# Normalising an attention head and adding it to the residual: one VectorE product and one GpSimd addition against eight fused VectorE operations

## What is computed

```
q, k, v = x @ Wq + bq, x @ Wk + bk, x @ Wv + bv            # (b, n, 8 heads, 64)
scores  = einsum('bihd,bjhd->bhij', q, k) / sqrt(64) + mask
weights = softmax(scores, axis=-1)
out     = einsum('bhij,bjhd->bihd', weights, v).reshape(b, n, 512)
x       = layernorm(x + out)
```

## Time and profile before

| | us |
|---|---|
| median of 3 runs | 2533.32 (2531.81 to 2533.53) |
| profiled execution, its own time | 2532.79 |
| its span, first to last instruction | 2530.8 |
| PE busy | 2431.8 (96%) |
| DVE busy | 2215.7 (88%) |
| POOL busy | 1474.6 (58%) |
| ACT busy | 1331.1 (53%) |
| clock granted to PE, mean | 0.982 |

### The profile page before, as it was taken

One profiled execution on the slowest core, in us unless ns is written; L12 is line 12 of the kernel. 1 busy time (PEld: TensorE's weight loads), 2 busy tenths in 40 slices (PEclk: granted clock), 3 DMA queues, 4 the chain that ended last, 5 costly groups with the idle time before them and its releaser, 6 DMA issues. The chain is left out here.

```text
span 2530.8 us, 55069 instructions
## 1 busy us (share of the span) xinstructions
PE 2431.8 (96%) x15497; PEld 2070.5 (82%) x15497; DVE 2215.7 (88%) x6933; ACT 1331.1 (53%) x4104; POOL 1474.6 (58%) x1806
## 2 busy tenths in 40 slices
PE   4899999999999999999999999999999999999983
PEld 3688888888888888888888888888888888888873
DVE  6889889889999999998998988988999999998862
ACT  3355555555555555555555555555555555555542
POOL 5655566566565665655656656656656566565531
PEclk7899999999999999999999999999999999999996
DMA  4255666666566666666566566666666666666564
GB/s 130 59 130 138 141 139 139 140 138 141 137 140 138 141 140 141 136 143 145 129 141 145 134 144 141 138 141 139 141 137 137 141 140 139 139 138 140 129 127 100
DMA packets 1382908, 342.56 MB, mean 135 GB/s; under 512 B 1084880, under 2 KB 1347152, under 8 KB 1382864
## 3 DMA queue, kind: packets, MB, share of 16 engines
q1 hardware_dynamic: 1382864, 342.05, 59.4%
HBM read 174.13 MB, written 167.77 MB: 135 GB/s over the span
## 5 line engine op out<-in xcount | busy, mean ns | idle before, releaser
L901 PE MATMUL rot<-w_hi,y_hi 128*128 128x512 f32 x1024 | 416.3, 407 | 2.7 <-DVE y_lo L818 2.0
L903 PE MATMUL rot<-w_hi,y_lo 128*128 128x512 f32 x1024 | 404.1, 395 | 0.0
L902 PE MATMUL rot<-w_lo,y_hi 128*128 128x512 f32 x1024 | 402.7, 393 | 0.0
L508 ACT ACTIVATE probs<-score,sc_nmax 128x128 f32<-128x128 f32 x1024 | 361.3, 369 | 27.4 <-DVE sc_nmax L671 23.5
L381 POOL TENSOR_TENSOR ve<-mv,eps_col 128x1 f32<-128x1 f32 (+1 forms) x448 | 130.2, 291 | 345.1 <-DVE mv L663 247.7
L411 POOL TENSOR_TENSOR x2b<-x,bias 128x512 f32<-128x512 f32 x128 | 165.9, 1296 | 265.5 <-DVE x L762 265.5
L671 DVE CUSTOM_DVE_ANT_0 score<-score,mask 128x128 f32<-128x128 f32 x1024 | 259.6, 315 | 1.3 <-PE score L1000 1.3
L406 POOL TENSOR_TENSOR x<-x,o_norm 128x512 f32<-128x512 f32 x128 | 165.5, 1293 | 156.1 <-DVE o_norm L716 156.1
L693 DVE CUSTOM_DVE_ANT_0 dot_tmp<-x,u 128x512 bf16<-128x512 f32 x256 | 244.8, 992 | 11.8 <-ACT x L615 7.3
L421 POOL TENSOR_SCALAR e<-e 128x512 f32<-128x512 f32 x128 | 246.3, 1924 | 13.7 <-ACT e L568 13.7
L386 POOL TENSOR_TENSOR rs<-ve,half_neg 128x1 f32<-128x1 f32 (+1 forms) x448 | 249.2, 570 | 0.6
(11 more groups left out here) (119 smaller groups left out, 7051.8 us busy)
## 6 DMA issues: line engine op xcount, KB each, us to landing
pt_hbm<-probs SPq DMA_DIRECT2D x512, 128.0 KB, 2.8
probs_t<-pt_hbm SPq DMA_DIRECT2D x128, 512.0 KB, 4.0
x_in<-in_x SPq DMA_DIRECT2D x128, 256.0 KB, 4.0
xt_hbm<-x_b SPq DMA_DIRECT2D x512, 64.0 KB, 2.3
xt_f<-xt_hbm SPq DMA_DIRECT2D x128, 256.0 KB, 2.8
ot_hbm<-o_t SPq DMA_DIRECT2D x512, 64.0 KB, 1.9
o_norm<-ot_hbm SPq DMA_DIRECT2D x128, 256.0 KB, 2.7
out_x<-x SPq DMA_DIRECT2D x128, 256.0 KB, 2.4
```

Source lines behind the costliest of these rows:

```text
L508: ins = act.activation(probs[:, 0, c, t, :], score_tile(c, g, h), ACT.Exp, bias=sc_nmax[:, c, t:t + 1], scale=-1.0, accum_out=sc_sum[:, pa ...
L901: pe.matmul(outp, lh, rh, start=first, stop=False)
L902: pe.matmul(outp, lh, rl, start=False, stop=False)
L903: return pe.matmul(outp, ll, rh, start=False, stop=last)
```

## The change

The product (L716) and the addition (L406) become eight `scalar_tensor_tensor` operations on DVE, one for each graph and head of the slot: x4 = o_norm * sc_inv[column i] + x4 over 64 features. They stand where L716 stood; POOL no longer takes part. DVE now waits for `x4_init` (in one slot of two), and gives `x4_done`; the reciprocal waits for that in place of `o_norm_done`, which is gone. The second edit puts 100 waits (`LOOP_SHIFT`) on a semaphore that has long been set into the start of DVE's program, ahead of the first products; they move everything behind them to higher addresses.

```diff
+LOOP_SHIFT = 100
...
             def emit(slot):
-                if slot.on(L_ON):
-                    k, first = slot.part(L_ON), slot.buf(L_ON, BUFS) // GROUP * GROUP
-                    res = x4[:, first:first + GROUP, k * CHUNKS * P:(k + 1) * CHUNKS * P]
-
-                    slot.wait(pool, o_norm_done, L_ON)
-                    if k == 0:
-                        slot.wait(pool, x4_init, L_ON - (GROUP - 1))
-                    pool.tensor_tensor(res, res, o_norm[:, :, :], ALU.add).then_inc(x4_done, 1)
...
+            for _ in range(LOOP_SHIFT):
+
+                dve.wait_ge(adj_in, 16)
...
                 if slot.on(L_ON):
-                    heads = o_norm[:, :, :].rearrange("p g (c d) -> p (g c) d", d=HEAD)
+                    k, first = slot.part(L_ON), slot.buf(L_ON, BUFS) // GROUP * GROUP
 
                     slot.wait(dve, ot_in, L_ON, each=16)
                     slot.wait(dve, inv_done, L_ON)
-                    dve.tensor_tensor(heads, heads,
-                                      sc_inv[:, :].unsqueeze(2).to_broadcast([P, CHUNKS * TILES, HEAD]),
-                                      ALU.mult).then_inc(o_norm_done, 1)
+                    if k == 0:
+                        slot.wait(dve, x4_init, L_ON - (GROUP - 1))
+                    for i in range(CHUNKS * TILES):
+                        g, at = i // TILES, i % TILES * HEAD
+                        res = x4[:, first + g, k * CHUNKS * P + at:k * CHUNKS * P + at + HEAD]
+                        ins = dve.scalar_tensor_tensor(out=res, in0=o_norm[:, g, at:at + HEAD], scalar=sc_inv[:, i:i + 1],
+                                                       in1=res, op0=ALU.mult, op1=ALU.add)
+                    ins.then_inc(x4_done, 1)
...
-                    slot.wait(dve, o_norm_done, L_PV, 1)
+                    slot.wait(dve, x4_done, L_PV, 1)
```

## The result

The changed kernel takes 2590.57 us (median of four, 2589.43 to 2591.65) against 2533.43 us for the kernel before on the same chip: a ratio of 1.0224 [1.0208, 1.0241], 2.2% slower. The forecast was no change, 2532.6 us, and the range ended at 2576. What happened is rival 2, at a higher price than its own.

The account below looks back on a forecast made before the run. PE was taken to set the pace, busy 2222.80 of 2225.00 us. The profiled 2532.79 + 0 + 0 + 0 - 0.7 gave 2532.1, and the median, 0.5 above, 2532.6 us; range 2528 to 2576.

Parts of the forecast that it names:

- rival 2: DVE's loop no longer fits what is held of the program: 0 to 1.9 us a turn, 2572 us; chance 0.27.
- the 0 that the sum has for the loop: In the loop, PE is never late despite DVE's added work and the collision: 0 us.
- four blocks may well be held: Argument against a fetch in each turn of DVE's loop, estimated to touch four blocks; nothing showed how many are held.
- The eight operations: On DVE in each slot: 0.165 us each, 1.32 for eight, less 0.60 for L716, so +0.72; bounds +0.48 and +1.64.
- The Trainium skill's two prices: For the eight on DVE: 58 cycles plus columns, 1.02 us, or columns plus 151 cycles, 1.79; the timelines favoured the first.
- The collision with L480: In the storing slot POOL's L480 gets in between the eight and DVE waits up to 1.29 us; lower bound 0.
- Margins of PE: In the storing slot DVE is 2.06 us late at y1_lo against 2.93, and 0.93 late at k with 0.98 remaining.
- Rival 1: DVE becomes the bound of the storing slot from 0.22 us per operation; upper bound +54 us, 2587 us; chance 0.13.
- The 0.67 behind L805: DVE's idle time late in the storing slot, ahead of y2_lo, was to swallow L805's remaining delay of 0.23 us.
- The forecast for this was 0.3: DVE's idle time in the loop was to fall from 3.0 to about 0.3 us a pair of slots.
- Start, end and POOL: Waits at DVE's start cost 0; last chain from L716 to the statistics gains 0.7 us; relieving POOL gains 0 in the loop.

Follow-up runs that it names:

- e1_shift200: The changed kernel with 200 waits in place of 100 at the start of DVE's program: 2538.87 us, ratio 1.0019.
- e3_before_shift160: The kernel before with nothing changed but 160 waits at the start of DVE's program: 2591.15 us, ratio 1.0218.
- e2: The changed kernel without its 100 waits, the fused operations alone: 2627.97 us, ratio 1.0374.
- e8: The changed kernel with 150 waits in place of 100: 2537.93 us, ratio 1.0014.
- e6_two_ops: The changed kernel without its waits, the eight fused operations replaced in all slots by a product and an addition on DVE: 2533.09 us, ratio 0.9995.
- e7_extra4: The kernel of e5_hybrid with four more fused operations of 64 columns in each slot of the loop, ahead of the eight: 2618.04 us, ratio 1.0332.
- e5_hybrid: The changed kernel without its waits, with two DVE operations replacing the eight only in the slots ahead of the loop: 2535.87 us, ratio 1.0007.
- e4: The kernel before with the change's 100 waits at the start of DVE's program and nothing else: 2534.62 us, ratio 0.9998.

## Why the prediction was wrong, point by point

**The step that failed** is the 0 that the sum has for the loop, under the assumption that the loop still runs from what is held of the program. It measured 55.5 us, 2.05 in each of 27 turns. Rival 2 described the case in full (packets all through the loop, DVE idle ahead of the transposition once in four slots), and gave it 0.27. e1_shift200 and e3_before_shift160 show it from both sides: the change without the fetching is 2538.9, the fetching without the change 2591.2.

Two things were wrong in its weighing. First, "four blocks may well be held" was taken as the likelier. By the reading of the packets above four are indeed held, and it did not help, because the block that follows the loop is fetched as well and makes a fifth; the fetches of the start, each a block ahead of where DVE is, could have shown this. The boundaries, estimated from the times of these fetches, stand in the later expectations some 13 instructions too high, which did not matter for the changed kernel (it reaches 19 to 24 ahead of one boundary and some 50 behind another) but made two expectations wrong, e2 and e8. Second, its price: 1.4 us a turn, from a fetch of 1.9. The instruction behind the branch came 2.6 us late and the second dot product ended 3.0 late, the 0.7 of the collision in it; 1.13 of this was slack, and 27 turns of 2.05 are the 55.5. Against e1_shift200, which has the same operations and turns of 75.26 us, a turn is 1.97 longer, which is what PE's weight load waits for; the other 0.09 of the 2.05 is what e1_shift200 has over the kernel before. The shortest DMA on another queue was a lower bound for this one and stood as the price.
The Trainium skill (Runtime: NRT & Kernel Launch, Instruction fetch mechanics) says that a taken branch whose target is outside what is held forces a fetch before execution goes on. The trace agrees, with 2.90 us against 0.29 from the branch to the next register instruction. It gives blocks of 16 KiB, two of them held at a time. The packets here are 8 KB, and four of these would be the page's 32 KiB; that four are held is a reading of this trace and not a measurement.

**The eight operations.** 0.165 was taken, 0.135 to 0.28 allowed; 0.196 was measured, +0.97 us a slot and not +0.72. The extrapolation took 1.04 ns a column from 512 down to 64, but L798's 0.23 fell only to 0.196 with 64 columns fewer.
The Trainium skill's two prices (VectorE: DVE Perf Modes, the section on the TRN2 errata) would have been 1.02 and 1.79 us for the eight; 1.57 lies between, nearer to the second, and the advice to minimise the number of operations was right here: in e6_two_ops two operations take 1.32.

**The collision with L480** was there as described, once in each storing slot, for 1.05 us where 1.29 was put. e6_two_ops shows it too, with a single gap.

**Margins of PE.** With the measured sizes the delay at y_lo is (0.97 - 0.67) + 0.97 + 1.05 = 2.32 and within the 2.93; only e7_extra4 shows PE waiting for y_lo, 1.4 us in all. At k it is 2.32 - 0.88 - 0.25 = 1.19, and against 1.91 (1238.25 less 1236.34) this looked safe. It was the wrong reader. In PE's code the wait for k stands one step ahead of the scores, before the products of L988, because they write a bank that k is read from. DVE and PE's weight loads in the kernel before, a storing slot whose transposition starts at 1227.76:

```profile
1236.27 0.70 DVE L777 STREAM_TRANSPOSE x_b<-x 128x512 f32<-128x512 f32 x1
```

```profile
1237.04 1.08 PEld L988 LDWEIGHTS rot<-adj_t,x 128*128 128x128 f32 x8
```

and in e5_hybrid, a storing slot whose transposition starts at 1230.62:

```profile
1239.82 0.70 DVE L787 STREAM_TRANSPOSE x_b<-x 128x512 f32<-128x512 f32 x1
```

```profile
1240.02 0.97 PEld L998 LDWEIGHTS rot<-adj_t,x 128*128 128x128 f32 x8 [0.15 <-issue]
```

DVE is through with k when it starts the transposition of x. That was 8.51 us into the slot and is now 9.20; PE loads the first weights at 9.28 and now at 9.40, 0.20 behind k and after a short wait. So the margin was 0.77 with the signal in it, and it is gone. This is the 0.24 us that PE waits for k in e5_hybrid, once in a turn, and why nearly all that is added beyond is paid in e7_extra4. Rival 1's point, put at a pitch of 0.22, is in fact at or just below 0.196: the fused operations stand on it. Over the loop that costs 2.8 us (e5), so "no change" would have been right for the fused operations (ratio 1.0007), but with nothing left over.

**Slack.** The 0.67 behind L805, which was to swallow the rest, is the wait for the scores, and e7 shows that it does not shrink: 0.73 a pair with DVE as the bound. Summed from the records of 400 to 2200 us, DVE's idle time went from 3.43 us a pair to 1.03 in e5; of its waits there 0.7 are of this kind. The forecast for this was 0.3.

**Start, end and POOL.** The 100 waits are free (e4: 0.9998), 200 are not (4.4 us at the first product). Of the 0.7 put on the end, 0.37 shows between the first of the eight and the statistics (1.69 against 2.06): the eight take 1.65 us and not 1.32. The whole part behind the last branch varies by more than that between runs. POOL's 183 us gained nothing.

## What to carry to other kernels

Before adding instructions to a loop on an engine, count where it begins and ends in that engine's instruction stream, prologue included, and look for packets on the instruction queue inside the loop; here ten waiting instructions more or less ahead of the loop decided 55 us, whether the new operations were in it or not. If such a stall shows, try the loop at another place (a shorter prologue is free, waits cost once they outlast the idle time at the start) before judging the change itself. When you work out how late a result may come, look for the first instruction that waits for it, which may be one that only reuses its buffer, and do not count a wait as slack when what it waits for is itself fed by the engine that waits.

## What the runs showed of the hardware

- DVE's program comes in packets of 8 KB, which lie 128 instructions apart. Loops that touch three blocks run without a fetch (seven kernels, up to 347 instructions), loops that touch four fetch five packets a turn (five kernels, from 303 instructions on). The switch lies between 692 and 702 for the first instruction, between 951 and 957 for the last.
- A branch to a block that is no longer held costs DVE 2.3 to 2.4 us of idle time in four of these five kernels, 3.6 in e2_shift0, where two packets are asked for at the branch.
- By the times of the packets the next block is asked for when DVE enters one, so that four are held and a loop on four blocks fetches five (a reading, not a measurement).
- A scalar_tensor_tensor of 128x64 with a column of scalars starts 0.196 us behind its predecessor, though it lasts 0.274.
- An operation of DVE with two inputs in SBUF that meets a POOL operation of 1.29 us loses 0.97 to 1.09, at the first gap between two such operations: one gap (e6) is as good as seven.
